# Expert tiles of 128 rows in place of 256 in a gated cross-attention and mixture-of-experts kernel

## The chip, the core and the metric

The kernel runs on one core of a Trainium2 chip. The metric is the device time of one execution in microseconds (us). TensorE multiplies, VectorE (DVE) and ScalarE (ACT) work element by element, GpSimd (POOL) does masks and issues indirect transfers, SyncE (SP) issues the other transfers. Each engine has a sequencer that takes the instructions in order, computes addresses that are held in registers, waits for semaphores and hands the work to the engine.

## What is computed

32 sequences of 128 tokens with 256 features pass a causal cross-attention with 16 heads (each gated and added to its input), then a mixture of experts: the router keeps the two best of eight experts for each token, every expert is a two-layer network of hidden width 1024 with an exact GELU, and the two results are weighted and added.

```python
x = x + tanh(g_xattn[0]) * xattn(layernorm(x), ctx, ctx, w_q, ..., b_o)
xf = layernorm(x).reshape(-1, 256)
logits = xf @ Wr + br
topv, _ = lax.top_k(logits, 2)
weights = softmax(where(logits >= topv[:, 1:2], logits, -inf))
h = gelu(einsum('td,edh->eth', xf, W1) + b1[:, None, :])
expert_out = einsum('eth,ehd->etd', h, W2) + b2[:, None, :]
x = x + tanh(g_ffn[0]) * einsum('etd,te->td', expert_out, weights)
```

## The kernel before, in words

The program has two blocks. The first (to about 456 us) does attention and routing for 16 groups of two sequences. For every token it scatters two rows into a DRAM table, `token_rows`: each expert has a region of it, and a row holds the normalized token in two fp16 parts (value and rest), its eight gates and its number. Behind each expert's last row a padding row is written often enough to fill a tile. A small table on one partition then says for each tile which expert it belongs to (`tile_expert`) and where its rows start (`tile_row`). The first block also issues the loads of the first two tiles and ends with a meeting of all engines.

The second block, `experts`, runs 39 tiles of 256 rows, which is enough for 8192 chosen rows and eight partly filled tiles. The loop over the tiles is written out (`pipeline`, `peeled`): i is a number in the program, but the tile's expert is only known on the chip. So `expert_of` (L1219) loads it from `tile_expert` into a register, and every weight address `wts[:, ds(expert, 1), at:at + ...]` is computed from that register by the sequencer. TensorE's iteration i (L1351 to 1388) loads the experts of tiles i and i+1, then does layer 1 of tile i+1 and layer 2 of tile i:

- Layer 1 (L1369): eight chunks c of 128 hidden features, six matmuls each: two halves of the 256 features times three products of the fp16 parts. The weight block of 128 x 128 is the stationary operand and the rows of the tile are the moving one, so a matmul moves 256 columns. Four different weight addresses occur in a chunk. The result of two chunks fills a PSUM bank, four banks hold a tile.
- Layer 2 (L1385): for each half of 128 rows 24 matmuls, in which the split GELU values are stationary and 256 columns of the second weight move. There are 16 different weight addresses; both halves use the same ones.

ScalarE applies GELU to layer 1 (L1285) into the one buffer `hf` and, for the tile before, the gate to the result (L1295, `yg`). VectorE splits `hf` in two fp16 parts (L1316, L1317, `hh`) and, after that, scales layer 2 and adds the bias (L1327, `yb`). GpSimd adds the gated rows to the output with an indirect DMA per 128 rows (L1259), each waiting for the one before, since two rows of a token must not be added at once. SyncE loads the rows of tile i+2 (L64 to 71: four transposing DMAs, one for each part and half of the features, and one for gates and numbers), in a ring of eight buffers, and the weights of experts 4 to 7 (L78) between the first tiles' rows; those of experts 0 to 3 have stayed in SBUF.

Of the kernel before, what the change touches and what calls it, by code (L numbers as in the profile page):

```python
# [12 lines left out]
P = 128  # L13
# [26 lines left out]
TILE = 2 * P  # L40
# [5 lines left out]
RING = 8  # L46
X_SCALE = 1024.0
# [4 lines left out]
def padding(eng, env, experts):  # L52

    eng.wait_ge(env["pad_rows_ready"], 1)
    for e in experts:
        place = eng.value_load(env["padplace"][0:1, e:e + 1], min_val=0, max_val=E * REG)
        eng.dma_start(env["xs_dram"][bass.ds(place, TILE), :].rearrange("(h p) r -> p h r", h=2),
                      env["padrow"][:, :].unsqueeze(1).to_broadcast([P, 2, ROW])).then_inc(env["pads_in"], 16)


def load_rows(sp, env, where, xh, j):
# [4 lines left out]
    for part in range(2):  # L66
        for k in range(KC):
# [3 lines left out]
    sp.dma_start(env["gates"][j][:, :, :], rows[:, D:].rearrange("(h p) r -> p h r", h=2)  # L71
                 ).then_inc(env["row_in"][j], 16)
# [38 lines left out]
def bass_flamingo(nc, x, ctx_in, g_xattn, g_ffn, w_q, b_q, w_k, b_k, w_v, b_v, w_o, b_o,  # L111
# [4 lines left out]
    with ExitStack() as stack:  # L116
# [53 lines left out]
        past = sb("past", [1, MAIN_TILES, E])  # L170
        te, ts = sb("te", [1, MAIN_TILES]), sb("ts", [1, MAIN_TILES])
        tile_no_int = te[:, :].bitcast(I32)
        tile_expert, tile_row = sb("tile_expert", [1, ALL_TILES], I32), sb("tile_row", [1, ALL_TILES], I32)

# [4 lines left out]
        first_xh = [sb(f"xh{i}", [P, 2, KC, TILE], F16) for i in range(2)]  # L179
        gates = [sb(f"gates{i}", [P, 2, ROW - D]) for i in range(RING)]  # L180
# [9 lines left out]
def attention_and_routing(nc, env):  # L190
# [11 lines left out]
    with ExitStack() as stack:  # L202
# [22 lines left out]
        cover = [env["first_xh"][i // 2][:, i % 2, :, :].rearrange("p k t -> p (k t)").bitcast(BF16)  # L225
# [133 lines left out]
        with nc.Block() as block:  # L359

            @block.sync
            def _(sp):
# [6 lines left out]
                def it(g, par, half, stays, stayed):  # L369
# [22 lines left out]
                    if isinstance(g, int) and g == -2:  # L392
# [23 lines left out]
                        for half in range(2):  # L416
                            at = E * REG + half * P
                            load(xs_dram[at:at + P, :], padrow[:, :])
# [36 lines left out]
                sp.wait_ge(params, 16 * 10)  # L455
# [130 lines left out]
            def _(act):  # L586
# [12 lines left out]
                def it(g, par, half, stays, stayed):  # L599
                    g1, p1 = g + 1, 1 - par  # L600
                    for n in range(QUADS):
                        if isinstance(g, int) and g == -1 and n == 1:
                            act.wait_ge(first_params, 16 * 6)
                        if isinstance(g, int) and g == -1 and n == 2:
                            act.wait_ge(params, 16 * 10)
# [307 lines left out]
            def _(pe):  # L913
# [13 lines left out]
                def it(g, par, half, stays, stayed):  # L927
                    g1, p1 = g + 1, 1 - par
                    for n in range(QUADS):
# [68 lines left out]
                        if isinstance(g, int) and g == 0 and n == 0:  # L998
                            pe.wait_ge(params, 16 * 10)
# [148 lines left out]
def experts(nc, env):  # L1148
# [8 lines left out]
    with ExitStack() as stack:  # L1157
# [7 lines left out]
        xh = first_xh + [sb(f"xh{i}", [P, 2, KC, TILE], F16) for i in range(2, RING)]  # L1165
        hf = sb("hf", [P, HC, TILE])
        hh = [sb(f"hh{i}", [P, 2, HC, TILE], F16) for i in range(2)]
        yb = [sb(f"yb{i}", [P, 2, D]) for i in range(2)]
        yg = [sb(f"yg{i}", [P, 2, D]) for i in range(2)]
# [5 lines left out]
        added = [sem(f"added{i}") for i in range(2)]  # L1175
# [9 lines left out]
        def pipeline(eng, it, lo, hi):  # L1185
# [6 lines left out]
            rounds = (hi - 3 - first) // RING if hi > MAIN_TILES else 0  # L1192
            peeled(lo - 2, first)
# [31 lines left out]
        with nc.Block() as block:  # L1225

            @block.sync
            def _(sp):
                def it(i, m, there):
                    if there(2) and not (isinstance(i, int) and i < 0):  # L1230

                        j = i + 2
                        when(sp, before(j, RING), added[1], added_value(j - RING))
                        settled(sp)
                        load_rows(sp, env, tile_row[0:1, bass.ds(j, 1)], xh[(m + 2) % RING], (m + 2) % RING)
                    if isinstance(i, int) and i == -1:
# [12 lines left out]
            def _(pool):  # L1249
                def it(i, m, there):  # L1250
                    if there(0):

                        for half in range(2):
                            pool.wait_ge(yg_ready, i * 2 + half + 1)
                            when(pool, half == 1 or before(i, 1), added[1 - half],
                                 added_value(i if half == 1 else i - 1))
                            settled(pool)
                            numbers = gates[m][:, half, E:E + 1].bitcast(I32)
                            pool.indirect_dma_start(  # L1259
                                out=out[:, :], out_offset=bass.IndirectOffsetOnAxis(ap=numbers, axis=0),  # L1260
                                in_=yg[m % 2][:, half, :], in_offset=None, compute_op=ALU.add
                                ).then_inc(added[half], 16)

                def last(tiles):
                    for half in range(2):
                        pool.wait_ge(added[half], added_value(tiles - 1))
# [9 lines left out]
            def _(act):  # L1276
                def it(i, m, there):
                    if there(1):
                        e = expert_of(act, i + 1)
                        for quarter in range(4):  # L1280
                            act.wait_ge(h_psum, (i + 1) * 4 + quarter + 1)

                            when(act, before(i + 1, 1), split_ready, i * 4 + quarter + 1)
                            for c in (2 * quarter, 2 * quarter + 1):
                                last = act.activation(  # L1285
                                    hf[:, c, :], HB[quarter][:, c % 2 * TILE:(c % 2 + 1) * TILE],
                                    ACT.Gelu, bias=b1t[:, bass.ds(e, 1), c], scale=gscale[:, bass.ds(e, 1)])
                            last.then_inc(gelu_ready, 1)
                    if there(0):
# [3 lines left out]
                        when(act, before(i, 2), added[1], added_value(i - 2))  # L1293
                        for half in range(2):
# [137 lines left out]
```

## Time and profile before

| | |
|---|---|
| median of 3 runs | 907.57 us (907.29 to 908.5) |
| profiled execution | 904.24 us, span 902.5 us |
| attention and routing | 0 to about 456 us |
| expert tiles on TensorE | 470 to 881 us |
| busy over the span | PE 797.3, PEld 722.0, DVE 586.5, ACT 432.2, POOL 364.3 us |
| mean granted TensorE clock | 0.959 |

The profile is one execution. Times of a timeline are us from the span's start. PE is TensorE's matmuls and PEld its weight loads; a record of a matmul is longer than the distance to the next one, since they are pipelined. A name with a q behind it is the engine's sequencer: FUSED_REGOPS computes an address in registers, TENSOR_LOAD loads a register from memory. "out<-in" gives the tiles written and read, "xN" a count, the two numbers behind it in part 5 of the page are busy time in us and the mean of one in ns, then the idle time before the group and what ended it. A granted clock of 1.00 is full speed (2.4 GHz), 0.50 half.

### The profile page before, as it was taken

Reading aid. Unit: us, or ns where it says so; the run is one execution under the profiler, and the core shown is the slowest. Engines: PE = TensorE matmul, PEld = TensorE weight load, DVE = VectorE, ACT = ScalarE, POOL = GpSimd, SP = SyncE. Lnnn points to the kernel's source line nnn. Section 1 sums busy time; section 2 is a strip of 40 time slices with the busy share of each in tenths; the row PEclk is TensorE's granted clock in tenths of the full one; section 3 lists DMA queues with packets and bytes.
Section 4 is the critical chain, followed back from the end, with each engine's and each line's share of the span. In section 5 each row is a group of like instructions: output and inputs, shape, how many; then the busy total and the mean of one; then the engine's idle time right before and its main releaser. Section 6 shows DMA issues by size and latency. Waiting matters only on the chain. (4 is left out here: it accounts for less than half of the span.)

```text
span 902.5 us, 24791 instructions
## 1 busy us (share of the span) xinstructions
PE 797.3 (88%) x7316; PEld 722.0 (80%) x7317; DVE 586.5 (65%) x1453; ACT 432.2 (48%) x955; POOL 364.3 (40%) x397
## 2 busy tenths in 40 slices
PE   3399999999999999998319999999999999999990
PEld 3289888888898888898218888888888888888880
DVE  2268999999999999988706454555545455545440
ACT  2156556665565665665105444444444444444440
POOL 2134555555565565656400233232322333332232
PEclk9699999999999999999559999999999999999996
DMA  8776887777778899984449644434333334433222
GB/s 187 135 138 123 178 177 153 135 154 157 166 162 215 198 214 222 193 172 144 146 147 295 151 70 65 65 50 64 53 56 50 53 54 56 54 51 44 25 25 27
DMA packets 132876, 108.81 MB, mean 121 GB/s; under 512 B 67744, under 2 KB 126496, under 8 KB 130592
## 3 DMA queue, kind: packets, MB, share of 16 engines
q1 hardware_dynamic: 117376, 87.19, 45.1%
q0 software_dynamic: 14304, 19.15, 13.8%
q8 instruction: 58, 0.95, 0.5%
q10 hardware_dynamic: 1088, 1.11, 0.4%
q14 instruction: 50, 0.41, 0.2%
HBM read 36.60 MB, written 34.36 MB: 79 GB/s over the span
## 5 line engine op out<-in xcount | busy, mean ns | idle before, releaser
L1259 POOL DMA_INDIRECT out_rows<-yg,gates x78 | 126.6, 1623 | 317.6 <-issue 150.3
L1369 PE MATMUL bank<-xh,wts 128*128 128x256 f16 x1872 | 212.2, 274 | 24.2 <-issue 24.1
L1369 PEld LDWEIGHTS bank<-xh,wts 128*128 x1872 | 183.6, 98 | 46.9 <-issue 24.9
L1385 PE MATMUL bank<-wts,hh 128*128 x1872 | 210.6, 273 | 0.0
L1385 PEld LDWEIGHTS bank<-wts,hh 128*128 128x128 f16 x1872 | 183.2, 98 | 21.2
L1285 ACT ACTIVATE hf<-bank,b1t,gscale 128x256 f32<-128x256 f32 x312 | 154.8, 562 | 20.2 <-PE bank L1369 19.1
L532 POOL TENSOR_SCALAR_AFFINE_SELECT xh<-rowmax 128x512 bf16<-128x512 bf16 x128 | 94.3, 737 | 138.3 <-DVE rowmax L785 124.0
L1036 PE MATMUL bank<-va,probs 128*128 128x102 f32 x1024 | 138.9, 277 | 9.0 <-DVE ao L733 8.9
L1316 DVE TENSOR_SCALAR hh<-hf,hscale 128x512 f16<-128x512 f32 x156 | 77.9, 499 | 104.5 <-ACT hf L1285 102.2
L1036 PEld LDWEIGHTS bank<-va,probs 128*128 128x128 f32 x1024 | 125.5, 192 | 12.1 <-DVE ao L733 6.6
L1295 ACT ACTIVATE yg<-yb,gates 128x256 f32<-128x256 f32 x78 | 35.4, 501 | 199.7 <-DVE yb L1327 148.0
L1317 DVE SCALAR_TENSOR_TENSOR hh<-hf,hscale,hh 128x512 f16<-128x512 f32 x156 | 117.2, 751 | 5.6
L785 DVE TENSOR_REDUCE rowmax<-bank 128x4 bf16<-128x512 f32 x128 | 87.7, 686 | 21.9 <-PE bank L943 15.4
L616 ACT ACTIVATE probs<-bank 128x512 f32<-128x512 f32 x128 | 76.5, 598 | 45.2 <-PE bank L990 45.0
L1327 DVE SCALAR_TENSOR_TENSOR yb<-bank,yscale,b_all 128x512 f32<-128x512 f32 x39 | 29.3, 751 | 104.8 <-PE bank L1385 96.6
L943 PE MATMUL bank<-wts 128*128 128x128 bf16 x512 | 49.9, 220 | 27.0 <-DMA wts<-queries 23.7
L544 POOL DMA_INDIRECT token_rows<-pay,slots x64 | 65.9, 1030 | 18.3 <-issue 11.3
L990 PE MATMUL bank<-wts 96*128 96x128 bf16 x512 | 73.1, 220 | 0.0
L988 PE MATMUL bank<-negident,xh 128*128 128x128 bf16 x512 | 72.8, 219 | 0.3 <-POOL xh L532 0.3
L943 PEld LDWEIGHTS bank<-wts 128*128 128x128 bf16 x512 | 39.3, 100 | 32.8 <-issue 29.8
L990 PEld LDWEIGHTS bank<-wts 96*128 96x128 bf16 x512 | 50.1, 98 | 1.8
L988 PEld LDWEIGHTS bank<-negident,xh 128*128 128x128 bf16 x512 | 49.8, 98 | 0.9 <-POOL xh L532 0.4
(168 smaller groups left out, 983.9 us busy)
## 6 DMA issues: line engine op xcount, KB each, us to landing
wts<-in_W SPq DMA_DIRECT2D x16, 1024.0 KB, 6.6
wts<-keys SPq DMA_DIRECT2D x96, 128.0 KB
wts<-queries SPq DMA_DIRECT2D x96, 128.0 KB
split_weights<-wts SPq DMA_DIRECT2D x8, 1024.0 KB, 5.2
wts<-split_weights SPq DMA_DIRECT2D x8, 1024.0 KB, 7.6
xin<-in_x SPq DMA_DIRECT2D x16, 256.0 KB, 2.8
cin<-in_ctx_in SPq DMA_DIRECT2D x16, 256.0 KB, 3.6
out_rows<-x SPq DMA_DIRECT2D x16, 256.0 KB
```

Of the source, the lines that this page charges most:

```text
L532: pool.affine_select(out=cover[n % 4][:, :, :], in_=rowmax[n % 2][:, :].unsqueeze(2).to_broadcast([P, 4, P]), compare_op=ALU.is_ge, fill=M ...
L785: dve.tensor_reduce(rowmax[n % 2][:, :], SB[n % 2][:, :].rearrange("p (a k) -> p a k", a=4), AX, ALU.max).then_inc(max_ready, 1)
L943: last = pe.matmul(ps[:, a * P:(a + 1) * P], qfull[par][:, h, tok], kfull[par][:, h, tok], start=True, stop=True)
L988: pe.matmul(ps[:, a * P:(a + 1) * P], cover[m % 4][:, a, :], negident[:, :], start=True, stop=False)
L990: last = pe.matmul(ps[:, a * P:(a + 1) * P], kst[i][:, h, tok], qst[i][:, h, tok], start=False, stop=True)
L1036: last = pe.matmul(OB[:, h * VA:(h + WIDE) * VA], probs[m % 4][:, a, :], va[i][:, b, h, :].unsqueeze(1).to_broadcast([P, WIDE, VA]), start ...
L1259: pool.indirect_dma_start(out=out[:, :], out_offset=bass.IndirectOffsetOnAxis(ap=numbers, axis=0), in_=yg[m % 2][:, half, :], in_offset=No ...
L1285: last = act.activation(hf[:, c, :], HB[quarter][:, c % 2 * TILE:(c % 2 + 1) * TILE], ACT.Gelu, bias=b1t[:, bass.ds(e, 1), c], scale=gscal ...
L1316: step(dve.tensor_scalar(high, full, hscale[:, bass.ds(e, 1)], None, ALU.mult))
L1317: dve.scalar_tensor_tensor(out=hh[b][:, 1, c, :].rearrange("p c t -> p (c t)"), in0=full, scalar=hscale[:, bass.ds(e, 1)], in1=high, op0=A ...
L1369: last = pe.matmul(HB[c // 2][:, c % 2 * TILE:(c % 2 + 1) * TILE], wts[:, bass.ds(expert[1], 1), at:at + P], xh[(m + 1) % RING][:, xp, k, ...
L1385: last = pe.matmul(YB[b][:, half * D:(half + 1) * D], hh[b][:, hp, c, half * P:(half + 1) * P], wts[:, bass.ds(expert[0], 1), at:at + D], ...
```

## The change

A tile has 128 rows. Since at most 127 rows of padding belong to an expert, 71 tiles are enough (9088 rows in place of 9984). Each tile has its own loads, its own pair of PSUM banks (two pairs take turns), one of two `hf` buffers and one scatter. The rows are loaded four tiles ahead. Waits go by halves of a tile's hidden features in place of quarters. The weights of experts 4 to 7 are issued one expert per iteration from iteration 0 on, each behind the rows of the tile four ahead. Work of the tile table that had tensors of its own uses part of the weight buffer. The core of the diff:

```diff
-TILE = 2 * P
+TILE = P
+AHEAD = 4
@@ padding
-        eng.dma_start(env["xs_dram"][bass.ds(place, TILE), :].rearrange("(h p) r -> p h r", h=2),
-                      env["padrow"][:, :].unsqueeze(1).to_broadcast([P, 2, ROW])).then_inc(env["pads_in"], 16)
+        eng.dma_start(env["xs_dram"][bass.ds(place, TILE), :], env["padrow"][:, :]).then_inc(env["pads_in"], 16)
@@ load_rows
-    sp.dma_start(env["gates"][j][:, :, :], rows[:, D:].rearrange("(h p) r -> p h r", h=2)
-                 ).then_inc(env["row_in"][j], 16)
+    sp.dma_start(env["gates"][j][:, :], rows[:, D:]).then_inc(env["row_in"][j], 16)
@@ experts, SyncE
-                    if there(2) and not (isinstance(i, int) and i < 0):
-                        j = i + 2
-                        when(sp, before(j, RING), added[1], added_value(j - RING))
+                    if there(AHEAD) and not (isinstance(i, int) and i + AHEAD < 2):
+                        j, k = i + AHEAD, (m + AHEAD) % RING
+                        when(sp, before(j, RING), added, added_value(j - RING))
                         settled(sp)
-                    if isinstance(i, int) and -1 <= i <= 1:
-                        for e in {-1: (EARLY,), 0: (EARLY + 1,), 1: range(EARLY + 2, E)}[i]:
-                            sp.wait_ge(weights_in, 16 * 2 * e)
-                            load_weights(sp, wts, w_dram, e, weights_in)
+                    if isinstance(i, int) and 0 <= i < E - EARLY:
+                        sp.wait_ge(weights_in, 16 * 2 * (EARLY + i))
+                        load_weights(sp, wts, w_dram, EARLY + i, weights_in)
@@ GpSimd
-                        for half in range(2):
-                            pool.wait_ge(yg_ready, i * 2 + half + 1)
...
+                        pool.wait_ge(yg_ready, i + 1)
+                        when(pool, before(i, 1), added, added_value(i - 1))
@@ ScalarE
-                        for quarter in range(4):
-                            act.wait_ge(h_psum, (i + 1) * 4 + quarter + 1)
-                            when(act, before(i + 1, 1), split_ready, i * 4 + quarter + 1)
-                            for c in (2 * quarter, 2 * quarter + 1):
+                        for half in range(2):
+                            act.wait_ge(h_psum, (i + 1) * 2 + half + 1)
+                            when(act, before(i + 1, 2), split_ready, (i - 1) * 2 + half + 1)
+                            for c in range(4 * half, 4 * half + 4):
                                 last = act.activation(
-                                    hf[:, c, :], HB[quarter][:, c % 2 * TILE:(c % 2 + 1) * TILE],
+                                    hf[b][:, c, :], HB[2 * b + half][:, c % 4 * TILE:(c % 4 + 1) * TILE],
@@ VectorE
-                        for quarter in range(4):
-                            c = slice(2 * quarter, 2 * quarter + 2)
+                        for half in range(2):
+                            c = slice(4 * half, 4 * half + 4)
@@ TensorE, layer 1
-                            when(pe, c % 2 == 0 and before(i + 1, 1), gelu_ready, i * 4 + c // 2 + 1)
+                            half = c // 4
+                            when(pe, c % 4 == 0 and before(i + 1, 2), gelu_ready, (i - 1) * 2 + half + 1)
                             for q, (wp, xp, k) in enumerate(terms):
                                 at = wp * 2048 + k * H + c * P
-                                last = pe.matmul(HB[c // 2][:, c % 2 * TILE:(c % 2 + 1) * TILE],
+                                last = pe.matmul(HB[2 * b + half][:, c % 4 * TILE:(c % 4 + 1) * TILE],
                                                  wts[:, bass.ds(expert[1], 1), at:at + P], xh[(m + 1) % RING][:, xp, k, :],
                                                  start=q == 0, stop=q == 5)
@@ TensorE, layer 2
-                        for half in range(2):
-                            for q, (hp, wp, c) in enumerate(terms):
-                                if half == 0 and q % 6 == 0:
-                                    pe.wait_ge(split_ready, i * 4 + q // 6 + 1)
-                                at = 4096 + wp * 2048 + c * D
-                                last = pe.matmul(YB[b][:, half * D:(half + 1) * D],
-                                                 hh[b][:, hp, c, half * P:(half + 1) * P],
-                                                 wts[:, bass.ds(expert[0], 1), at:at + D], start=q == 0, stop=q == 23)
+                        for q, (hp, wp, c) in enumerate(terms):
+                            if q % 12 == 0:
+                                pe.wait_ge(split_ready, i * 2 + q // 12 + 1)
+                            at = 4096 + wp * 2048 + c * D
+                            last = pe.matmul(YB[b][:, 0:D], hh[b][:, hp, c, :],
+                                             wts[:, bass.ds(expert[0], 1), at:at + D], start=q == 0, stop=q == 23)
```

## Rows read from the trace of the kernel before

**Rows 1.** Timeline of TensorE's weight loads, 697 to 712 us: start, duration, what.

```profile
697.55 5.23 PEld L1369 LDWEIGHTS bank<-xh,wts 128*128 x48
...
708.03 4.03 PEld L1369 LDWEIGHTS bank<-xh,wts 128*128 x37
```

**Rows 2.** Part 5 of the page: the two matmul groups of the expert stage.

```profile
L1369 PE MATMUL bank<-xh,wts 128*128 128x256 f16 x1872 | 212.2, 274 | 24.2 <-issue 24.1
...
L1385 PE MATMUL bank<-wts,hh 128*128 x1872 | 210.6, 273 | 0.0
```

**Rows 3.** Instructions by line, whole run (PEldq: TensorE's sequencer): ns min/median/max, first, last start.

```profile
L1369 PEldq FUSED_REGOPS  x1248: 46/46/51, 470.2 to 869.1; - x179
...
L1385 PEldq FUSED_REGOPS  x624: 46/46/60, 480.9 to 876.6; - x156
```

**Rows 4.** The same view of 470.2 to 471.7 us, ahead of the clock's rise.

```profile
L1369 PE MATMUL bank<-xh,wts x7: 390/421/421, 470.4 to 471.6; 128*128 128x256 f16 x7
...
L1369 PEldq FUSED_REGOPS  x12: 46/46/51, 470.2 to 471.6; - x12
```

**Rows 5.** The same view of 475 to 483.1 us: one iteration on TensorE's sequencer.

```profile
L1219 PEldq TENSOR_LOAD <-tile_expert x2: 306/310/314, 475.1 to 475.8; - x2
...
L1369 PEldq FUSED_REGOPS  x32: 46/46/51, 476.8 to 480.8; - x32
...
L1385 PEldq FUSED_REGOPS  x16: 46/46/60, 480.9 to 483.0; - x16
```

**Rows 6.** The same view in the middle of the stage, 697.4 to 708 us.

```profile
L1369 PEldq FUSED_REGOPS  x32: 46/46/51, 697.4 to 701.6; - x32
...
L1219 PEldq TENSOR_LOAD <-tile_expert x2: 301/354/407, 706.2 to 706.8; - x2
```

**Rows 7.** Timeline of matmuls of 128 columns with fresh weights, attention stage.

```profile
255.80 0.22 PE L988 MATMUL bank<-negident,xh 128*128 128x128 bf16 x1
...
256.21 0.22 PE L990 MATMUL bank<-wts 96*128 96x128 bf16 x1
```

**Rows 8.** One line's instructions, whole run: the transposing loads on SyncE's queue.

```profile
L69 SPq DMA_TRANSPOSE xh<-token_rows x156: 1126/1152/2412, 456.6 to 819.8; - x156
```

**Rows 9.** Timeline of the DMA issues on SyncE's queue, 504 to 520 us.

```profile
505.06 5.64 SPq L69 DMA_TRANSPOSE xh<-token_rows  x4
...
512.12 5.97 SPq L69 DMA_TRANSPOSE xh<-token_rows  x4
```

**Rows 10.** Timeline of the end of the span.

```profile
881.40 0.75 DVE L1327 SCALAR_TENSOR_TENSOR yb<-bank,yscale,b_all 128x512 f32<-128x512 f32 x1 [4.49 <-PE bank L1385]
882.28 0.91 ACT L1295 ACTIVATE yg<-yb,gates 128x256 f32<-128x256 f32 x2 [4.33 <-DVE yb L1327]
...
888.61 1.54 POOL L1259 DMA_INDIRECT out_rows<-yg,gates  x1 [2.83 <-issue]
893.27 1.54 POOL L1259 DMA_INDIRECT out_rows<-yg,gates  x1 [3.12 <-issue]
```

**Rows 11.** Timeline of ScalarE, VectorE and GpSimd around two iterations.

```profile
705.08 0.75 DVE L1317 SCALAR_TENSOR_TENSOR hh<-hf,hscale,hh 128x512 f16<-128x512 f32 x1
...
709.37 0.91 ACT L1295 ACTIVATE yg<-yb,gates 128x256 f32<-128x256 f32 x2 [5.14 <-DVE yb L1327]
710.23 1.94 ACT L1285 ACTIVATE hf<-bank,b1t,gscale 128x256 f32<-128x256 f32 x4
710.70 1.54 POOL L1259 DMA_INDIRECT out_rows<-yg,gates  x1 [4.23 <-ACT yg L1295]
```

**Rows 12.** Timeline of the seam between the two blocks, 456 to 471 us.

```profile
456.65 5.06 SPq L69 DMA_TRANSPOSE xh<-token_rows  x4
...
468.23 0.43 SPq L71 DMA_DIRECT2D gates<-token_rows  x1
```

**Rows 13.** Windows of TensorE: stretch, length, busy (instructions), granted clock, DMA share, GB/s.

```profile
400.00:430.00 30.00, 26.08 (x277) 1.00 0.52 163
430.00:440.00 10.00, 4.53 (x15) 0.62 0.22 82
```

More of the change, by code:

```diff
@@ L178, in bass_flamingo @@
         rows_placed, ties_in, row_in = sem("rows_placed"), sem("ties_in"), [sem(f"row_in{i}") for i in range(RING)]
-        first_xh = [sb(f"xh{i}", [P, 2, KC, TILE], F16) for i in range(2)]
-        gates = [sb(f"gates{i}", [P, 2, ROW - D]) for i in range(RING)]
+        first_xh = [sb(f"xh{i}", [P, 2, KC, TILE], F16) for i in range(4)]
+        gates = [sb(f"gates{i}", [P, ROW - D]) for i in range(RING)]
         bank = [stack.enter_context(nc.psum_tensor(f"bank{i}", [P, 512], F32)) for i in range(8)]
@@ L415, in it @@
                         load(out[T:T + P, :], padrow[:, 0:D])
-                        for half in range(2):
-                            at = E * REG + half * P
-                            load(xs_dram[at:at + P, :], padrow[:, :])
+                        load(xs_dram[E * REG:E * REG + TILE, :], padrow[:, :])
                     if there(g + 1):
@@ L1174, in experts @@
         row_in = env["row_in"]
-        added = [sem(f"added{i}") for i in range(2)]
+        added = sem("added")
         h_psum, gelu_ready, split_ready = sem("h_psum"), sem("gelu_ready"), sem("split_ready")
@@ L1251, in it @@
                     if there(0):
-                        for half in range(2):
-                            pool.wait_ge(yg_ready, i * 2 + half + 1)
[L1255 to L1262, printed above, removed]
+                        pool.wait_ge(yg_ready, i + 1)
+                        when(pool, before(i, 1), added, added_value(i - 1))
+                        settled(pool)
+                        numbers = gates[m][:, E:E + 1].bitcast(I32)
+                        pool.indirect_dma_start(
+                            out=out[:, :], out_offset=bass.IndirectOffsetOnAxis(ap=numbers, axis=0),
+                            in_=yg[m % 2][:, :], in_offset=None, compute_op=ALU.add).then_inc(added, 16)
                 def last(tiles):
-                    for half in range(2):
-                        pool.wait_ge(added[half], added_value(tiles - 1))
+                    pool.wait_ge(added, added_value(tiles - 1))
                 pipeline(pool, it, 0, MAIN_TILES)
@@ L1292, in it @@
                         act.wait_ge(yb_ready, i + 1)
-                        when(act, before(i, 2), added[1], added_value(i - 2))
-                        for half in range(2):
-                            act.activation(yg[m % 2][:, half, :], yb[m % 2][:, half, :], ACT.Copy,
-                                           scale=gates[m][:, half, bass.ds(e, 1)]).then_inc(yg_ready, 1)
+                        when(act, before(i, 2), added, added_value(i - 2))
+                        act.activation(yg[m % 2][:, :], yb[m % 2][:, :], ACT.Copy,
+                                       scale=gates[m][:, bass.ds(e, 1)]).then_inc(yg_ready, 1)
                 all_tiles(act, it)
@@ L1308, in it @@
                         b = (m + 1) % 2
-                        for quarter in range(4):
-                            c = slice(2 * quarter, 2 * quarter + 2)
-                            dve.wait_ge(gelu_ready, (i + 1) * 4 + quarter + 1)
-                            when(dve, quarter == 0 and before(i + 1, 2), y_psum, i)
+                        for half in range(2):
+                            c = slice(4 * half, 4 * half + 4)
+                            dve.wait_ge(gelu_ready, (i + 1) * 2 + half + 1)
+                            when(dve, half == 0 and before(i + 1, 2), y_psum, i)
                             high = hh[b][:, 0, c, :].rearrange("p c t -> p (c t)")
-                            full = hf[:, c, :].rearrange("p c t -> p (c t)")
+                            full = hf[b][:, c, :].rearrange("p c t -> p (c t)")
                             step(dve.tensor_scalar(high, full, hscale[:, bass.ds(e, 1)], None, ALU.mult))
@@ L1341, in _ @@
                         step(dve.tensor_scalar(tile_no[:, :], tile_no[:, :], float(MAIN_TILES), None, ALU.add))
-                        rows_of_tiles(dve, step, env, lo, min(lo + MAIN_TILES, ALL_TILES))
+                        rows_of_tiles(dve, step, table, lo, min(lo + MAIN_TILES, ALL_TILES))
                     dve.sem_inc(rest_ready, 1)
```

47 lines of the change are left out of this document (24 added, 23 removed).

## The prediction

> **What bounds the kernel now.** I read the windows of the engines first, then the groups of instructions, then the sequencer's instructions line by line, then SyncE's queue and the two ends. From 470 to 881 us the 39 expert tiles run. There TensorE starts a pair of weight load and matmul every 10.48/96 = 0.109 us, tile after tile without a hole: line 1369 begins at 697.55 and again at 708.03 [rows 1], and both groups show 1872 matmuls of 256 columns [rows 2]. So the array is the bound today, 39 x 10.48 = 409 us. What the groups of matmuls don't show is how near the next limit lies. The addresses of the weights depend on the tile's expert, which is in a register, so TensorE's sequencer computes them: 1248/39 = 32 register instructions per tile at line 1369 and 624/39 = 16 at line 1385 [rows 3]. They come at a fixed pace: 12 from 470.2 to 471.6 us, 0.127 apart, with the array at half clock (matmuls of 421 ns) [rows 4]; 32 from 476.8 to 480.8, 0.129 apart, with it at full clock [rows 5]. The same pace beside a slow and a fast array says that it is the sequencer's own: about 0.125 us each, with one and a half pairs handed over in that time, or 0.083 us a pair. One iteration, 475.1 to 483.1 us [rows 5]: two loads of the expert number with their checks and the waits, 475.1 to 476.8 (1.65 us); 32 register instructions of layer 1, to 480.9 (4.13); 16 of layer 2, to 483.1 (2.15). That is 7.95 us; the second half of layer 2 reuses the addresses and needs none. In the middle of the stage it is the same: 697.4 to 701.6 for the 32, loads at 706.2 and 706.8 [rows 6]. Under an array that takes 10.48 us this is hidden.
>
> **What the change does to TensorE's work.** Layer 2 keeps 24 matmuls of 256 columns per 128 rows: 71 x 24 = 1704 in place of 1872. Layer 1 keeps its 48 matmuls per tile, since the weights are the stationary operand; each now moves 128 columns and there are 71 x 48 = 3408. The array's price of such a pair: eight in a row from 255.80 to 256.21 us, 0.41/7 = 0.058 us apart [rows 7]. So a tile costs the array 48 x 0.058 + 24 x 0.109 = 5.40 us, 71 of them 383 us, 26 less than now. For the pair itself 0.058 is the lower bound and 0.109 [rows 1] the upper; a sequencer at 0.083 lies between and takes over.
>
> **What it does to the sequencer's work.** Everything that the sequencer does belongs to a tile, not to a row: eight chunks with four weight addresses each in layer 1, 16 addresses in layer 2, two loads of the expert number. The written-out loop recomputes all of it for each of 71 tiles. Gone are the 24 pairs that reused addresses, and two of four waits in each layer, worth some 0.1 us at most. A tile costs 1.65 + 4.13 + 2.15 = 7.93, taken as 7.95 us [rows 5]; the spread of the iterations (4.0 to 4.2 us between the first and last of the 32 [rows 5, 6]) and the missing waits make it 7.8 to 8.1. That is more than the array's 5.40, so the array can build no lead that lasts: it gains 24 x 0.109 - 2.15 = 0.5 us in layer 2 and loses it in the 1.65 us of loads, standing idle some 1 us per tile, and runs layer 1 at 0.083. The period is the sequencer's.
>
> By the Trainium skill (TensorE: Matmul & The Clock Gate, Back-to-back issue gap) a sustained stream of weight loads and matmuls of 128 columns runs at about 81 ns a pair, set by both operations; the eight of [rows 7] at 58 ns disagree, though eight is a short stream. It speaks against this change too and is a rival below. The skill (DMA: Bandwidth & Descriptors, Latency and other measured facts) also puts a register's load from memory at 600 ns or more; here it takes 306 to 314 ns [rows 5], and by the page's figure the sum would be 70 x 2 x 0.3 = 42 us longer.
>
> **The other engines, per tile of 128 rows, against 7.95 us.** SyncE's queue: now 4 transposing loads of 1.15 us each [rows 8] and a period of 512.12 - 505.06 = 7.06 us where it isn't held back [rows 9], 5.64 of it the four. Halved rows could halve them or leave them as they are: 4.2 to 7.1 us. I take 5 (a fixed part and one that scales); no transfer size but one is shown. All of it is under 7.95, and four tiles of lead cover the landing. If the array set the pace at 5.4, the upper end would not be covered. GpSimd: a scatter follows the one before after 4.66 us when they queue (888.61 to 893.27 [rows 10]); one per tile fits. ScalarE and VectorE form a ring (GELU of tile i+1, split, bias of tile i, gating of tile i, next GELU): GELU of 256 columns comes every (1.94)/4 = 0.48 us [rows 11], so 0.24 to 0.48 for 128 columns, taken as 0.36, eight are 2.9; a last split pair 1.25 (0.75 for the second of it, no more for the first), the bias step 0.5 (0.75 for twice the columns [rows 10]), the gating 0.46 (half of 0.91), four hand-overs of 0.13: 5.6 us (4.6 to 6.9). Hidden too. The second PSUM pair and second hf buy slack where there is slack already: zero, with the array's idle microsecond as cover. SyncE's wait for the scatter of tile j-8 ahead of the rows of tile j has only later rows queued behind it, and that scatter is over some four periods before tile j is due: zero. The weights of experts 4 to 7 now stand behind the rows of tiles 4 to 7 on that queue; 71/8 = 9 tiles an expert put expert 4 at about tile 35: zero, up to 7 us an expert if it were due at once.
>
> **The ends.** At the seam SyncE issues the first two tiles' loads from 456.65 to 468.66 [rows 12] and TensorE follows; the eight transposes at 0.78 in place of 1.15 save 3 us (0 to 5). The longer table (71 entries) is VectorE's work of about 1 us more, ahead of 456.65, hidden behind the last rows' landing. At the end the bias step starts at 881.40, 0.2 after TensorE's end, but the last scatter only at 893.27, behind the one of 888.61 that itself waited [rows 10]. With one scatter per 7.95 us nothing queues: bias, gating, then the scatter 1.4 us after the gating starts (709.37 to 710.70 [rows 11]), that is at +2.4 us in place of +12.1 from TensorE's end. From the last scatter's start to the end of the span it stays 902.5 - 893.3 = 9.2, so 11.6 in all.
>
> **Sum.** The first iteration's header starts some 1.1 us ahead of its first register instruction (470.2 [rows 4]), so at 469.1 - 3 = 466.1; first layer 1, partly at the low clock, 5.5; 70 iterations x 7.95 = 556.5; last layer 2 with its load 3.7: TensorE ends at 1031.8. Tail 11.6: span 1043.4. The profiled execution of before has 904.24 for a span of 902.5, so 1045.1; the median is 3.3 above that: 1048 us, 15.5% slower. Own range, from 7.8 to 8.1 per tile (-11, +11) and the ends (+-5): 1030 to 1066.
>
> **Rivals.** (a) The array sets the pace, and 26 us of it are saved: the register instructions are slow only as recorded, or overlap with hand-over when the queue runs dry. For it: the profiled execution isn't slower than the others, so recording costs nothing visible, but under an array at 10.48 it would not be. Against: the fixed pace at both clocks [rows 4, 5]. Then the ring of 5.6 decides: 467 + 3.4 + 70 x 5.6 + 2.6 + 11.6 + 5 = 882, faster by 2.8%. It decides where the sequencer needs less than 5.6 a tile. Chance 8%. (b) Weight loads limit a long stream of short pairs, somewhere between 0.058 [rows 7] and 0.109 [rows 1], in the middle 0.083, and the sequencer's loads hide behind layer 2: 48 x 0.083 + 2.62 = 6.6, in all 467 + 5 + 462 + 2.6 + 11.6 + 5 = 953, slower by 5%; chance 5%. It decides where pairs take over 0.083 with the sequencer ahead; the eight of [rows 7] speak against it. The skill's rule named above is this mechanism; its 81 ns would give some 7 us less. (c) The idle microsecond per tile lets the clock fall to its 1.2 GHz level, where pairs take twice as long: 48 x 0.116 + 24 x 0.218 = 10.8 us a tile, in all 467 + 5.6 + 756 + 5.2 + 11.6 + 5 = 1250 us. Busy 26.08 of 30 us kept 1.00, 4.53 of 10 did not [rows 13]; here about 6.9 of 7.95 would be busy, like the first. Chance 7%, part of it as single dips. That fewer padded rows (9984 to 9088) bring the time down is right for the array only, and is in (a).
>
> **Chances.** Forecast 0.80, (a) 0.08, (b) 0.05, (c) 0.07. Range: the forecast's own with some dips of the clock above and a cheaper hand-over below, 1005 to 1090. 0.2% is about what a measurement of this kernel can tell from no change: faster 0.07, same 0.01, slower 0.92.
>
> **What the profile after would show.** Register instructions 71 x 32 = 2272 and 71 x 16 = 1136 on TensorE's sequencer at 0.125 us; tile period 7.95 us; layer-1 matmuls in bursts averaging 0.083 apart; an idle gap "issue" of about 1 us ahead of each layer 1, granted clock 1.00; scatters 7.95 us apart; ScalarE waiting for TensorE in every tile. A period near 5.5 would prove me wrong on the sequencer, one near 6.5 points to (b), a clock of 0.5 to (c).

## The result and the profile after

The kernel with tiles of 128 rows takes 1052.06 us in the median of 4 runs (1049.64 to 1053.38), beside 908.04 (907.29 to 909.1) before: 1.160 times the time, 95% interval 1.157 to 1.164. Slower by 144 us. The profiled execution is one of the four, 1053.38 us with a span of 1051.5.

The page of after, its span, busy times, clock row and the chain that ended last:

```profile
span 1051.5 us, 30913 instructions
...
PE 896.6 (85%) x8684; PEld 758.3 (72%) x8685; DVE 582.3 (55%) x1457; ACT 493.3 (47%) x1204; POOL 347.6 (33%) x390
...
PEclk9799999999999999759999999999999999999998
...
PE 45%; issue 6%; DMA 2%; SPq 2%; POOL 0%; ACT 0%; DVE 0%; DVEq 0%; POOLq 0%; ACTq 0%
```

TensorE is shown busy for 100 us longer than before, though the array has fewer columns to move: a record of a short matmul lasts 224 ns in the mean while the next one starts some 84 ns later, so such records cover gaps, and this number doesn't tell that the array waits. "issue" in the chain is time in which nothing that the profile shows was waited for. The groups of the expert stage (lines are those of after: 1365 is layer 1, 1380 layer 2, 1282 the GELU) answer to [rows 2]:

```profile
L1365 PE MATMUL bank<-xh,wts 128*128 128x128 f16 x3408 | 304.0, 224 | 82.8 <-issue 80.2
L1365 PEld LDWEIGHTS bank<-xh,wts 128*128 x3408 | 238.1, 97 | 158.6 <-issue 106.4
L1282 ACT ACTIVATE hf<-bank,b1t,gscale 128x128 f32<-128x128 f32 x568 | 213.9, 457 | 171.2 <-PE bank L1365 171.2
...
L1380 PE MATMUL bank<-wts,hh 128*128 x1704 | 201.4, 274 | 3.7 <-issue 0.9
```

There are 3408 matmuls of 128 columns and 1704 of 256, as counted in the prediction. Ahead of layer 1 TensorE stands idle with "issue" for 80 us in all. The timeline of TensorE's weight loads answers to [rows 1]:

```profile
703.60 2.56 PEld L1380 LDWEIGHTS bank<-wts,hh 128*128 128x128 f16 x24 [0.15 <-issue]
707.43 4.05 PEld L1365 LDWEIGHTS bank<-xh,wts 128*128 x48 [1.26 <-issue]
711.66 2.56 PEld L1380 LDWEIGHTS bank<-wts,hh 128*128 128x128 f16 x24 [0.18 <-issue]
715.24 0.47 PEld L1365 LDWEIGHTS bank<-xh,wts 128*128 x6 [1.02 <-issue]
```

Layer 1 starts at 707.43 and again at 715.24, a period of 7.81. The mean is a little longer: the second tile's layer 1 starts at 474.55 and the last one's at 1028.89 in TensorE's timeline, (1028.89 - 474.55)/69 = 8.03. The 48 loads of layer 1 take 4.05 us, 0.084 each, then 24 of layer 2 take 2.56 at 0.107, and then comes a hole of 1.0 to 1.3 us. In the instructions by line, this is what the sequencer does (and, in the last row, SyncE's transposing loads, which answer to [rows 8]):

```profile
L1365 PEldq FUSED_REGOPS  x2272: 46/46/51, 468.5 to 1032.9; - x190
...
L1380 PEldq FUSED_REGOPS  x1136: 46/46/60, 478.6 to 1038.0; - x190
...
L1220 PEldq TENSOR_LOAD <-tile_expert x142: 294/302/490, 467.4 to 1035.3; - x142
...
L69 SPq DMA_TRANSPOSE xh<-token_rows x284: 1093/1141/2421, 455.0 to 990.2; - x142
```

2272 = 71 x 32 and 1136 = 71 x 16 register instructions, 142 loads of the expert number, all per tile. The window of 600 to 800 us (length, then busy time and instructions of PE, PEld, DVE, ACT and POOL, granted clock, DMA share, GB/s) shows full clock and engines that all have time (the granted clock is 1.00 from 480 to 1030 us):

```profile
600.00:800.00 200.00, 176.97 (x1796) 139.23 (x1794) 73.28 (x125) 87.45 (x224) 38.58 (x25) 1.00 0.26 37
```

The waits (us in all, times, longest) say who waits for whom; line 1257 is the scatter:

```profile
POOL out_rows L1257 <- ACT yg L1291: 439.3, 64, 31.5
...
ACT hf L1282 <- PE bank L1365: 171.2, 140, 2.0
...
PE bank L1365 <- issue: 80.2, 70, 21.4
```

GpSimd waits for ScalarE, ScalarE for TensorE's layer 1, and TensorE for "issue", nothing that the profile shows; that this is its own sequencer is for the experiments to show. The end of the span answers to [rows 10]:

```profile
1033.28 2.56 PEld L1380 LDWEIGHTS bank<-wts,hh 128*128 128x128 f16 x24 [0.22 <-issue]
...
1036.12 2.56 PEld L1380 LDWEIGHTS bank<-wts,hh 128*128 128x128 f16 x24 [0.29 <-issue]
...
1038.24 1.54 POOL L1257 DMA_INDIRECT out_rows<-yg,gates  x1 [6.52 <-ACT yg L1291]
...
1039.76 0.51 ACT L1291 ACTIVATE yg<-yb,gates 128x256 f32<-128x256 f32 x1 [2.34 <-DVE yb L1323]
1042.96 1.54 POOL L1257 DMA_INDIRECT out_rows<-yg,gates  x1 [3.17 <-DMA out_rows<-yg,gates]
```

### The profile page after: what moved, and what is told of

It is laid out like the page before. It is cut to its first block, busy times and chain, and to the rows that moved or that the text cites. A ratio compares the mean times of both kernels' runs of the same rounds, so it can differ in the third digit from the quotient of the medians.

```text
span 1051.5 us, 30913 instructions
## 1 busy us (share of the span) xinstructions
PE 896.6 (85%) x8684; PEld 758.3 (72%) x8685; DVE 582.3 (55%) x1457; ACT 493.3 (47%) x1204; POOL 347.6 (33%) x390
## 4 chain that ended last, share of the span: by engine, by line
PE 45%; issue 6%; DMA 2%; SPq 2%; POOL 0%; ACT 0%; DVE 0%; DVEq 0%; POOLq 0%; ACTq 0%
PE bank L1365 27%; PE bank L1380 18%; DMA wts<-split_weights 2%; SPq L69 1%; DMA out_rows<-yg,gates 0%; POOL out_rows L1257 0%; SPq L71 0%; SPq L64 0%; SPq L77 0%; ACT yg L1291 0%; DVE yb L1323 0%; SPq L1238 0%; DVEq L1323 0%; POOLq L1184 0%; SPq L1184 0%
## 5 line engine op out<-in xcount | busy, mean ns | idle before, releaser
L1365 PE MATMUL bank<-xh,wts 128*128 128x128 f16 x3408 | 304.0, 224 | 82.8 <-issue 80.2
L1365 PEld LDWEIGHTS bank<-xh,wts 128*128 x3408 | 238.1, 97 | 158.6 <-issue 106.4
L1282 ACT ACTIVATE hf<-bank,b1t,gscale 128x128 f32<-128x128 f32 x568 | 213.9, 457 | 171.2 <-PE bank L1365 171.2
L1257 POOL DMA_INDIRECT out_rows<-yg,gates x71 | 109.7, 1545 | 482.5 <-ACT yg L1291 439.3
L1312 DVE TENSOR_SCALAR hh<-hf,hscale 128x512 f16<-128x512 f32 x142 | 69.0, 486 | 358.6 <-ACT hf L1282 358.5
L1380 PE MATMUL bank<-wts,hh 128*128 x1704 | 201.4, 274 | 3.7 <-issue 0.9
L1380 PEld LDWEIGHTS bank<-wts,hh 128*128 128x128 f16 x1704 | 160.4, 98 | 34.4 <-issue 12.9
L1313 DVE SCALAR_TENSOR_TENSOR hh<-hf,hscale,hh 128x512 f16<-128x512 f32 x142 | 106.7, 751 | 5.1
L785 DVE TENSOR_REDUCE rowmax<-bank 128x4 bf16<-128x512 f32 x128 | 87.6, 685 | 19.5 <-PE bank L943 13.0
L943 PE MATMUL bank<-wts 128*128 128x128 bf16 x512 | 50.1, 221 | 22.8 <-DMA wts<-queries 19.5
L797 DVE SCALAR_TENSOR_TENSOR wts<-wts,wnow 128x512 f16<-128x512 f32 (+1 forms) x64 | 47.5, 745 | 0.0
```

The source lines that it names most:

```text
L785: dve.tensor_reduce(rowmax[n % 2][:, :], SB[n % 2][:, :].rearrange("p (a k) -> p a k", a=4), AX, ALU.max).then_inc(max_ready, 1)
L943: last = pe.matmul(ps[:, a * P:(a + 1) * P], qfull[par][:, h, tok], kfull[par][:, h, tok], start=True, stop=True)
L1257: pool.indirect_dma_start(out=out[:, :], out_offset=bass.IndirectOffsetOnAxis(ap=numbers, axis=0), in_=yg[m % 2][:, :], in_offset=None, co ...
L1282: last = act.activation(hf[b][:, c, :], HB[2 * b + half][:, c % 4 * TILE:(c % 4 + 1) * TILE], ACT.Gelu, bias=b1t[:, bass.ds(e, 1), c], sca ...
L1313: dve.scalar_tensor_tensor(out=hh[b][:, 1, c, :].rearrange("p c t -> p (c t)"), in0=full, scalar=hscale[:, bass.ds(e, 1)], in1=high, op0=A ...
L1365: last = pe.matmul(HB[2 * b + half][:, c % 4 * TILE:(c % 4 + 1) * TILE], wts[:, bass.ds(expert[1], 1), at:at + P], xh[(m + 1) % RING][:, x ...
```

## The experiments

Each was run beside the kernel before on the same chip, whose median was 905.57 to 907.91 us there (908.04 beside after). The kernel after wasn't run again with them; differences to it are to its 1052.06 us. Two theories stand against each other at first: the period of 8.0 us is the sequencer's (register instructions, loads and waits, one after another), or it belongs to the array's short pairs or to the small steps per tile of another engine.

**Fixed addresses in the kernel after, a_static.**

```diff
-                        expert[0] = expert[1] if m > 0 and not isinstance(i, int) else expert_of(pe, i)
-                        expert[1] = expert_of(pe, i + 1)
...
-                        pe.wait_ge(weights_in, expert[1] * (16 * 2) + 16 * 2)
+                        pe.wait_ge(weights_in, 16 * 2)
...
-                                                 wts[:, bass.ds(expert[1], 1), at:at + P], ...
+                                                 wts[:, 0:1, at:at + P], ...
...
-                                             wts[:, bass.ds(expert[0], 1), at:at + D], ...
+                                             wts[:, 0:1, at:at + D], ...
```

> The kernel after, but TensorE takes the weights of expert 0 for every tile, at addresses fixed in the program: no register instructions and no loads of the expert number on its sequencer. (The output is therefore not the mixture; the arithmetic per tile is the same.) My theory (the sequencer sets the period of 8.05 us): the period falls to the next bound. That is SyncE's queue, since the trace of after shows the transposing load at 1.14 us as before although it has half the rows: 6.4 us a tile without and about 7 us with contention, 71 tiles, so some 945 to 985 us. Rival 1 (short pairs take 0.083 us in the array itself whoever hands them over): layer 1 stays at 4.0 us, a tile at 6.6 to 7, and the pairs in layer 1 stay 0.083 apart. Rival 2 (something per tile outside TensorE, such as the scatter, sets 8.05): no change, 1052 us.

Measured: 974.78 us (974.08 to 975.47), 77 below after. In its timelines, first TensorE's matmuls, then its weight loads (line 1361 is layer 1 here):

```profile
704.54 2.84 PE L1361 MATMUL bank<-xh,wts 128*128 128x128 f16 x48 [1.87 <-DMA gates<-token_rows]
707.22 2.78 PE L1376 MATMUL bank<-wts,hh 128*128 128x256 f16 x24
710.86 2.84 PE L1361 MATMUL bank<-xh,wts 128*128 128x128 f16 x48 [0.86 <-DMA gates<-token_rows]
```

```profile
704.51 2.69 PEld L1361 LDWEIGHTS bank<-xh,wts 128*128 128x128 f16 x48 [2.12 <-issue]
```

Layer 1 now takes 2.69 us for 48 loads, (2.69 - 0.10)/47 = 0.055 us a pair, and layer 2 follows at once. So the array takes short pairs at 0.055 us in a long stream too, as [rows 7] had shown for eight; that the pace of after was the array's is refuted. The hole ahead of layer 1 is a different one now: it ends with the landing of rows. SyncE's queue and the row of the waits:

```profile
703.86 4.96 SPq L69 DMA_TRANSPOSE xh<-token_rows  x4
709.02 0.42 SPq L71 DMA_DIRECT2D gates<-token_rows  x1
710.27 5.90 SPq L69 DMA_TRANSPOSE xh<-token_rows  x4
```

```profile
PE bank L1361 <- DMA gates<-token_rows: 90.6, 63, 4.4
```

SyncE needs 6.41 us from this tile's loads to the next one's (703.86 to 710.27): four issues of 1.14 us, the gates, and the loads of the row number in between. In the mean it is more, since some issues take up to 2.5 us, as in the group that took 5.90:

```profile
L69 SPq DMA_TRANSPOSE xh<-token_rows x284: 1098/1141/2468, 456.1 to 947.5; - x142
```

The last group of four starts at 943.64, so (943.64 - 456.1)/70 = 6.96 us a tile, and layer 1 starts 6.92 us apart in the mean. 70 x (8.03 - 6.92) = 78 us is the measured gain of 77; with 6.41 it would have been 113. In this stage SyncE waits for no other engine. Its queue is the next bound.

**The same edit in the kernel before, b_static.**

> The kernel before with the same edit (expert 0 for every tile, addresses fixed in the program, so the output isn't the mixture). My theory: with 256 rows the array is the bound at 0.109 us a pair, so the sequencer's work is hidden and the time stays within 0.5% of 908 us. If the sequencer's part showed already before, it would fall by more than 1%.

Measured: 903.84 us, ratio 0.998 (0.995 to 1.000). Under tiles of 256 rows the sequencer's work is hidden, all of it or all but 0.5% of the time.

**One load of the number less, or one more, in the kernel after: a_oneload and a_extraload.**

```diff
-                        expert[0] = expert[1] if m > 0 and not isinstance(i, int) else expert_of(pe, i)
+                        kept = isinstance(i, int) and expert.get("of") == i
+                        expert[0] = expert[1] if kept or (m > 0 and not isinstance(i, int)) else expert_of(pe, i)
                     if there(1):
                         expert[1] = expert_of(pe, i + 1)
+                        expert["of"] = i + 1 if isinstance(i, int) else None
```

```diff
                     if there(1):
+                        expert_of(pe, i + 1)
                         expert[1] = expert_of(pe, i + 1)
```

> The kernel after, but TensorE keeps the register of tile i+1 for the next iteration in place of loading the number again: one load with its check, 0.64 us, less in 70 iterations. My theory: every bit of the sequencer's work shows, the period falls from 8.05 to 7.41, in all by 45 us to 1007. Rival (the sequencer has slack and the matmuls' own pace counts): no change or only part of it.

> The kernel after with one load of the expert number more per iteration on TensorE's sequencer. My theory: 0.64 us more in each of 71 iterations, 45 us, 1097. Rival (slack): less than half of that.

Measured: 1005.31 us (1003.51 to 1007.11), 47 less, and 1100.29 (1097.29 to 1103.28), 48 more. Expected were 45 each way. Weight loads of a_oneload:

```profile
700.10 4.07 PEld L1367 LDWEIGHTS bank<-xh,wts 128*128 x48 [0.46 <-issue]
...
707.38 4.16 PEld L1367 LDWEIGHTS bank<-xh,wts 128*128 x48 [0.52 <-issue]
```

The period is 7.28, the layers take as long as before, and only the hole has shrunk, from 1.0 to 1.3 us to 0.5. Part of both differences lies ahead of the tiles: in the profiled executions the first layer 1 starts at 465.29 in a_oneload, at 468.64 in after and at 474.07 in a_extraload, though the first block is the same. Between starts of layer 1 the period goes from 8.03 to 7.37 and to 8.67 (means), so one load is worth 0.66 and 0.63 us, against 0.64 expected. A cost that shows in full in both directions has no slack around it.

**One load more in the kernel before, b_extra1** (the same edit as the second of these).

> The kernel before with one load of the expert number more per iteration on TensorE's sequencer (0.64 us with its check). By throughput there is room: a tile needs some 8 us of the sequencer and 10.48 of the array, so a first theory gives no change (within 0.3%). Mine: what counts is how long the array can live on what is queued while the sequencer is in its loads. In the trace of before the first load of an iteration starts at 706.20 and the array's next layer 1 at 708.03, 1.83 us later, of which the loads and waits take 1.69. So 0.64 more exceeds that lead by 0.5 us in each of 39 iterations: 19 us, about 926 us (+2.1%).

Measured: 927.38 us (924.81 to 936.4), ratio 1.026 (1.019 to 1.032), 19.5 us more: clear of no change, not clear of 2%. Weight loads:

```profile
702.12 5.23 PEld L1387 LDWEIGHTS bank<-wts,hh 128*128 128x128 f16 x48
708.10 5.15 PEld L1371 LDWEIGHTS bank<-xh,wts 128*128 x48 [0.75 <-issue]
...
719.16 2.86 PEld L1371 LDWEIGHTS bank<-xh,wts 128*128 x27 [0.68 <-issue]
```

Periods of 11.06 (708.10 to 719.16) in place of 10.48, with a hole ahead of each layer 1 that wasn't there. Of the 0.63 to 0.66 us that a load costs, 19.5/39 = 0.50 a tile shows by the times and 0.57 by the mean period of the trace (11.05), so some 0.1 to 0.15 was covered. The sequencer has time for it in the sum (7.95 + 0.7 against 10.48), and yet the array runs dry: what is queued for it when the header starts lasts for the 1.65 us of the header [rows 5] and 0.1 to 0.15 more, an estimate of 1.7 to 1.8 us. The kernel before stands that close to the edge.

**No loads of rows behind tile 7, a_norows.**

```diff
-                    if there(AHEAD) and not (isinstance(i, int) and i + AHEAD < 2):
+                    if isinstance(i, int) and 2 <= i + AHEAD < RING:
...
-                    return (i - m) * (16 * LOADS // RING) + 16 * LOADS
+                    return 16 * LOADS
```

> The kernel after without the loads of rows behind tile 7: tiles 8 to 70 compute again on the rows in the ring's buffers (so the output is wrong in those, the work per tile the same). My theory (the sequencer): no change, 1052 us within 0.5%. Rival (SyncE's queue or the transfers share in the 8.05 us): faster by over 1%.

Measured: 1052.96 us (1052.08 to 1053.84), no change. Layer 1 starts at the same distance (weight loads):

```profile
707.33 4.14 PEld L1365 LDWEIGHTS bank<-xh,wts 128*128 x48 [1.19 <-issue]
...
715.36 1.66 PEld L1365 LDWEIGHTS bank<-xh,wts 128*128 x19 [1.16 <-issue]
```

**Both edits together, a_norows_static.**

> The kernel after with both: no loads of rows behind tile 7, and expert 0's weights at addresses fixed in the program, no loads of the number on TensorE's sequencer (output wrong, work per tile on the engines the same). What is left are the array (48 x 0.056 + 24 x 0.109 = 5.3 us) and the ring of ScalarE and VectorE (estimated 5.6, 4.6 to 6.9). I expect 5.6 us a tile: 468.6 + 3.5 + 70 x 5.6 + 2.6 + 12.9 + 2 = 882 us. If the sequencer were still felt in another way, or the short pairs took 0.083 (6.6 us a tile), it would be 950 or more.

Measured: 897.09 us, ratio 0.988 (0.986 to 0.991). A full round of its timeline:

```profile
703.85 2.90 ACT L1282 ACTIVATE hf<-bank,b1t,gscale 128x128 f32<-128x128 f32 x8 [0.24 <-issue]
...
706.78 0.48 DVE L1312 TENSOR_SCALAR hh<-hf,hscale 128x512 f16<-128x512 f32 x1
...
707.30 0.75 DVE L1313 SCALAR_TENSOR_TENSOR hh<-hf,hscale,hh 128x512 f16<-128x512 f32 x1
708.15 0.48 DVE L1323 SCALAR_TENSOR_TENSOR yb<-bank,yscale,b_all 128x256 f32<-128x256 f32 x1
708.77 0.51 ACT L1291 ACTIVATE yg<-yb,gates 128x256 f32<-128x256 f32 x1 [2.02 <-DVE yb L1323]
...
709.52 2.90 ACT L1282 ACTIVATE hf<-bank,b1t,gscale 128x128 f32<-128x128 f32 x8 [0.24 <-issue]
```

Gating, eight GELUs, last split pair, bias, gating, next GELU: 703.85 to 709.52, 5.67 us, and TensorE's layer 2 waits for VectorE's split. It is the ring of the prediction (5.6). Eight GELUs of 128 columns take 2.90 us, 0.35 each. The time is 15 us above the expectation. 70 x 0.07 explains 5 of it. The other 10 stand near the start of the stage, where TensorE's layer 1 waits for rows to land:

```profile
501.77 5.28 PE L1361 MATMUL bank<-xh,wts 128*128 128x128 f16 x48 [4.11 <-DMA gates<-token_rows]
...
511.70 2.84 PE L1361 MATMUL bank<-xh,wts 128*128 128x128 f16 x48 [1.81 <-DMA gates<-token_rows]
```

Four tiles (478.9 to 511.7) take 32.8 us in place of 4 x 5.67 = 22.7, while the weights of experts 4 to 7 are loaded too (the transfer engines are 90% busy and move 273 GB/s from 500 to 520 us). In that window the granted clock is 0.83 in the mean: behind the wait of 4.11 us layer 1 takes 5.28 us in place of 2.84. Right behind them, to 550 us, six tiles take 5.30 each, the array's own pace (forecast 5.40), until the ring holds TensorE. Under the 8 us of after the same loads cost nothing: its tiles there take 7.9 to 8.1.

**A third of TensorE's pairs left out, a_fewpairs.**

```diff
-                        terms = [(wp, xp, k) for wp, xp in ((0, 0), (0, 1), (1, 0)) for k in range(KC)]
+                        terms = [(wp, xp, k) for wp, xp in ((0, 0), (1, 0)) for k in range(KC)]
...
-                        terms = [(hp, wp, c) for half in range(2) for hp, wp in ((0, 0), (1, 0), (0, 1))
+                        terms = [(hp, wp, c) for half in range(2) for hp, wp in ((0, 0), (0, 1))
...
```

> The kernel after without a third of TensorE's matmuls: layer 1 leaves out the product of the first part of the weights with the second part of the rows (16 of 48 pairs), layer 2 the second part of the hidden values (8 of 24 pairs); so the output is less exact. The register instructions stay 32 and 16 a tile, since the left-out pairs used addresses that are computed anyway. Two readings of the sequencer's pace differ here. If a register instruction costs 0.124 us by itself and pairs are handed over in its shade: no change, 1052 us within 0.5%, a third of TensorE's work gone for nothing. If the hand-over of pairs at 0.083 us is what takes the time: 24 x 0.083 = 2.0 us less a tile, 141 us, 911 us.

Measured: 1047.69 us (1046.75 to 1048.62), 4 below after: 24 of 72 pairs a tile left out, and 0.4% gained (2.5 us of it ahead of the tiles: the first layer 1 starts at 466.13 in the profiled execution, at 468.64 in after). The weight loads, the register instructions of layer 1 and TensorE's window from 600 to 800 us (length, busy, granted clock, DMA share, GB/s):

```profile
703.16 4.03 PEld L1365 LDWEIGHTS bank<-xh,wts 128*128 x32 [1.49 <-issue]
707.50 2.00 PEld L1380 LDWEIGHTS bank<-wts,hh 128*128 128x128 f16 x16 [0.31 <-issue]
711.13 4.16 PEld L1365 LDWEIGHTS bank<-xh,wts 128*128 x32 [1.63 <-issue]
```

```profile
L1365 PEldq FUSED_REGOPS  x2272: 46/46/51, 466.0 to 1026.0; - x190
```

```profile
600.00:800.00 200.00, 166.33 (x1206) 0.90 0.27 37
```

32 loads of layer 1 now take 4.03 us, as 48 did; the register instructions are the same 2272, and in both kernels their starts lie 0.124 us apart in the median. The mean period falls only from 8.03 to 7.97. So it is the register instructions that take the time, and pairs are handed over in their shade. The same can be read off the program: in each chunk of after one, three, one and one pairs stand between the register instructions, which nevertheless follow one another at the same 0.124 to 0.125 us, with a longer gap now and then (0.132 in the mean). A side result: TensorE got a mean clock of 0.90 in this window, lost for some stretches, and the time didn't rise, because the array isn't what is waited for.

**Tiles of 256 rows, empty ones left out, b_skip.** The table's last cumulated count says how many tiles hold rows, at least 32; with this input it is 36 of 39. Tiles 32 to 38 stand in a branch on each engine, on TensorE one around layer 1 of the next tile and one around layer 2 of this one: 7 x 2 = 14.

```diff
+SURE = 2 * T // TILE
...
+    step(dve.tensor_scalar(env["tied"][:, :], mostint[:, :], 2.0, 64.0, ALU.is_gt, ALU.mult))
+    dve.tensor_tensor(env["usedint"][:, :], env["tied"][:, :], small[0:1, 5, E - 1:E], ALU.add).then_inc(table_ready, 1)
...
+        @contextmanager
+        def if_used(eng, i):
+            if isinstance(i, int) and SURE <= i < MAIN_TILES:
...
+                with eng.If(used["n"] > i):
+                    yield
...
+                        with if_used(pe, i + 1):
...
+                        with if_used(pe, i):
```

> The kernel before with its tiles of 256 rows, in which tiles 32 to 38 are worked on only if they hold rows: the table's last cumulated tile count is written to a register's source, and each engine jumps over a tile that lies beyond it. With this input 36 of the 39 tiles hold rows. Theory: what costs the array is whole tiles of padding, and they can be left out without another instruction per row: 3 x 10.48 = 31.4 us less, some 0.3 to 1 us for each of the 14 branches on TensorE back (4 to 14 us), so 880 to 891 us, faster than both. Rival: a jump empties the sequencer's lead each time (over 2 us each), and the gain is gone.

Measured: 876.74 us beside 907.91, ratio 0.968 (0.962 to 0.975), faster than both. TensorE's matmuls at the last tiles, around which the branches stand (1400 is layer 1, 1419 layer 2):

```profile
826.30 5.40 PE L1400 MATMUL bank<-xh,wts 128*128 128x256 f16 x48
831.54 5.40 PE L1419 MATMUL bank<-wts,hh 128*128 x48
836.78 5.40 PE L1400 MATMUL bank<-xh,wts 128*128 128x256 f16 x48
842.02 10.64 PE L1419 MATMUL bank<-wts,hh 128*128 x96
```

From tile to tile it is still 10.48 us (826.30 to 836.78), with a branch ahead of each part, and the two last layer 2 (x96) follow one another without a gap across a layer 1 that is jumped over. Those branches, nine of the 14, cost the array nothing; the other five stand behind its last matmul and have no array work to delay. The gain of 31.2 us (by the interval 23 to 34) is that of three tiles, 31.4.

## Why the prediction was right, point by point

- **The bound.** The forecast was the sequencer at 7.95 us a tile; after shows 8.03. a_oneload and a_extraload show that its work counts in full, a_norows and a_fewpairs that SyncE's and the array's don't, a_static that without it the tile is shorter. Read from a trace in which it was hidden [rows 4 to 6], the size was right within 0.1 us, and 70 x 0.08 = 5.6 us is most of the 8.1 that separate 1051.5 from the forecast span of 1043.4; 1.3 more come from the seam (the first load of the number at 467.4 in place of 466.1), the rest from the end. Two of the waits fell away and yet the 32 instructions took no less (about 4.3 us with small gaps every eight or so, against the 4.13 that I took); the middle of the stage, 697.4 to 701.6 plus one, would have been the better row. Half of the 8.1 us was made good by luck: the forecast put the median 3.3 above the profiled execution, and in after it lies 1.3 below it, so that 1048 missed 1052 by only 4.
- **A wrong word in a right sum.** The prediction spoke of pairs handed over at 0.083 us. a_fewpairs shows that a third fewer pairs take as long (4.03 and 4.05 us) and that the register instruction's 0.124 is what counts. The sum was made of register instructions, so it stood.
- **The array** at 0.058 for a short pair: 0.055 in a stream of 48 (a_static). Rival (b), and with it the Trainium skill's 81 ns (TensorE: Matmul & The Clock Gate, Back-to-back issue gap), is refuted here: that would have been 3.9 us for what took 2.69. That layer 1 of after ran at 0.084 is a coincidence of the two numbers. The 600 ns of the Trainium skill for a register's load (DMA: Bandwidth & Descriptors, Latency and other measured facts) is twice the 0.30 us of its record in after, and near the 0.63 to 0.66 that a load with its check is worth there.
- **SyncE's queue.** This term was mis-sized: I took 0.78 us for a transposing load of half the rows and 5 for a tile; it takes 1.14 in the median (1.15 before) and 6.96 where nothing holds the queue back (a_static). Hidden under 8 us it cost nothing there, but at the seam the saving of 3 us didn't come. The second block's first layer 1 started at 468.6 in place of 470.4 because the loads began at 454.99 in place of 456.65; why, wasn't tried. It need not be the change: among the seven kernels with after's first block the first layer 1 starts anywhere from 465.29 to 474.07.
- **ScalarE and VectorE** as estimated: 0.35 us a GELU (0.36), the ring 5.67 (5.6).
- **The end.** The tail was forecast at 11.6 us. The last two layer 2 run back to back (1033.28 and 1036.12), since the last iteration has no layer 1, so the last scatter waits for the one of 1038.24 and starts at 1042.96, some 4.1 us behind TensorE's end and not 2.4; the queue was gone as expected, all but that. The difference is under 2 us.
- **Rival (a)**, the array's 26 us: it needs the sequencer's cost gone and SyncE's too. With both gone (a_norows_static) the kernel is 1.2% faster than before, and then the ring is the bound. **Rival (c)**, the clock: 1.00 in after from 480 us on. a_fewpairs has a mean of 0.90 in the expert stage without a loss of time.

What stays open is the small gaps among the register instructions (0.3 us a tile).

## What to carry to other kernels

A program whose matmul addresses come from a register has a second pace to keep: each different address cost its sequencer the same time here (0.124 us), whether the matmuls behind it moved 128 or 256 columns. Before cutting tiles in half, count what each engine's sequencer does per tile and put it against the new, shorter array time; it can be read from a trace in which it is still hidden. If the aim is less padding, look first at how it is spread: here leaving out whole empty tiles gave 3.2% at no cost per row, where finer tiles lost 16%.

## What the runs showed of the hardware that I had not expected

- Register instructions on TensorE's sequencer start 0.124 us apart in the median though the record of one is 46 ns, and weight loads and matmuls are handed over meanwhile (a_fewpairs: 32 or 48 pairs in 4.03 and 4.05 us).
- Issuing a transposing DMA costs SyncE 1.14 us with 128 rows and 1.15 with 256 (medians; single ones up to 2.5).
- What is queued for the array lasts for an estimated 1.7 to 1.8 us of pairs of 256 columns; sequencer work of 2.3 us in one piece opens a hole even where the sequencer has time to spare on average (b_extra1).
- Nine conditional jumps on TensorE's sequencer, among or between its last tiles, left no mark on the array (b_skip).
